# Graph attention layers on one core: normed rows turned by VectorE blocks and a DRAM scratch instead of by TensorE

## The chip, the cores and the metric

The kernel runs on one core of one Trainium2 chip. The metric is the device time of one execution in microseconds (us). TensorE (PE) multiplies and loads its weights (PEld), VectorE (DVE) and ScalarE (ACT) work on SBUF and PSUM, GpSimd (POOL) on SBUF alone, and SyncE (SP) only issues transfers here.

## The reference

64 graphs of 128 nodes with 256 features. The input is normed and clipped at zero, goes through three attention layers, and is added to the result:

```python
h = jnp.maximum(_layernorm(x, axis=-1), 0.0)          # x: (64, 128, 256)
x = h
for l in range(3):
    si = x @ attn_w[l, :d];  sj = x @ attn_w[l, d:]
    scores = si[:, :, None] + sj[:, None, :] + attn_b[l]
    scores = jnp.where(scores >= 0, scores, 0.2 * scores)
    scores = jnp.where(mask, scores, -jnp.inf)        # mask: adjacency or diagonal
    attn = jax.nn.softmax(scores, axis=-1)
    agg = jnp.einsum('bij,bjd->bid', attn, x)
    h = layernorm(x + agg, g1[l], beta1[l])
    ff = jax.nn.gelu(h @ W1[l] + b1[l], approximate=False) @ W2[l] + b2[l]
    x = layernorm(h + ff, g2[l], beta2[l])            # W1: 256x1024, W2: 1024x256
return x_input + x
```

## The kernel before

The work is cut into 48 items: 16 groups of four graphs (512 rows), each through three layers. A batch is four groups; its four groups go through layer 0, then layer 1, then layer 2, so a batch has 12 items and there are four batches. Item q has layer `q % 12 // 4`.

Each engine runs a list written out by hand: a prologue for the first items, then `slot(s)` for s from 1 on, in which the engine does pieces of the items s-1 to s+4. Engines are tied by counting semaphores only, and each engine works strictly in the order of its list. The order around the change is set by these lists.

For one item: `j_dots` and `i_dots` (VectorE, L620 and L627) make sj and si; sj goes to a DRAM scratch (`send_sj`) and comes back as a row on all 128 partitions (`load_sj`, tile `sj_bc`). `masked` (L654) takes the minimum of that row and a penalty tile `pen` of plus or minus 1e30 made from the adjacency by `penalty` (L641). `leaky` (ScalarE, L842) adds si and applies the slope, `minus_max` (VectorE, L658) reduces the maximum, `exps` (ScalarE, L848) makes the exponentials E, `e_turn` (TensorE, L1000) transposes them into the PSUM bank `util`, `et_out` copies them out, `aggregate` (L969) multiplies with x into an accumulator, `attend` (VectorE, L667) divides by the sum and adds x. `moments1` and `norm1` (L674, L517, L519, L680) norm the rows; between them GpSimd makes the reciprocal root as a power (`make_rstd`, L389). `z1_turn` (TensorE, L990) transposes the normed rows into `util` in two halves of four transposes. `h_high` (ScalarE) scales and shifts the half in place (`h_out`, L829) and rounds it to `ht_hi` (L836); `h_low` (VectorE, L685) makes the remainder `ht_lo`. The feed-forward part works in eight chunks: `ffn1(c)` (L940, 6 matmuls of 512 columns into one of three banks `hbank`), `gelu_high` (ScalarE, L813 and L819), `low` (VectorE, L541), `ffn2(c)` (L955, 12 matmuls of 256 columns into the accumulator). GpSimd makes gamma and beta times the normed rows (`h_gamma`, L409, `h_beta`, L416), VectorE adds them to the accumulator (`residual`, L555), norms (`moments2`, `norm2`, L562, L570), and GpSimd applies `x_gamma`, `x_beta` (L426, L434) and, in layer 2, `add_input` (L455). Items of layer 0 also need the input statistics (`input_moments`, L528, `input_shift`, L535) and `penalty`.

All eight PSUM banks are taken: three `hbank`, one `util`, and four `acc`, two for items of even q and two for those of odd q:

```python
acc = [psum(f"acc{i}", [P, HG, D]) for i in range(4)]
def acc_of(i, h): return acc[2 * (i.q % 2) + h]
```

So the aggregation of one item runs into the pair that ffn2 of the item before doesn't use. Weights are split in a high and a low part (`round_weights` on ScalarE, `split_weights`, L510, on VectorE) during the first items.

## Time and profile before

| | |
|---|---|
| Median of three runs | 1281.47 us (1281.34 to 1281.74) |
| The profiled execution, its own time | 1281.6 us |
| Its span, first to last instruction | 1279.8 us |
| Granted TensorE clock, mean | 0.997 |
| Busy: TensorE / weight loads | 1240.6 / 1122.5 us |
| Busy: VectorE / ScalarE / GpSimd | 1110.3 / 917.7 / 652.5 us |
| DMA | 52.31 MB, mean 41 GB/s |

The span leaves out what lies before the first and after the last instruction, 1.8 us here. Busy shares are means over the whole span. A matmul's duration reaches over the start of the next one, so the step from start to start, not the duration, is what a matmul costs.

### The profile page before, as it was taken

The numbers are of one execution on the slowest core, as the hardware profiler recorded it, in microseconds if no ns is written. First come the engines' busy times: TensorE is split into PE (matmuls) and PEld (weight loads), VectorE is DVE, ScalarE is ACT, GpSimd is POOL, SyncE is SP. The second block draws the span as 40 slices with busy tenths as digits, with TensorE's granted clock in tenths as the row PEclk, the third lists the DMA queues.
The fourth block names the chain that finished last, engine by engine and source line by source line (L and its number), as shares of the span: only waits on it lengthen the run. The fifth ranks groups of instructions, "written<-read, shape, count | busy, mean of one in ns | idle before, by whom it ended". The sixth has DMA issues, their size and how long they took to land.

```text
span 1279.8 us, 23042 instructions
## 1 busy us (share of the span) xinstructions
PE 1240.6 (97%) x7877; PEld 1122.5 (88%) x7877; DVE 1110.3 (87%) x3331; ACT 917.7 (72%) x1754; POOL 652.5 (51%) x535
## 2 busy tenths in 40 slices
PE   3899999999999999999999999999999999999997
PEld 1799999988899999999889999999989899989996
DVE  7888888899998788889998888789999888888765
ACT  4777777677876776678777776777778766776663
POOL 1435553556555534554566445544666355435563
PEclk9999999999999999999999999999999999999998
DMA  7111111112220001011230000002321100000111
GB/s 248 53 33 43 26 26 34 34 51 66 67 67 10 10 10 17 10 34 51 75 100 26 9 18 10 9 10 43 99 75 42 34 10 9 10 17 26 26 41 58
DMA packets 52944, 52.31 MB, mean 41 GB/s; under 512 B 9272, under 2 KB 45148, under 8 KB 52828
## 3 DMA queue, kind: packets, MB, share of 16 engines
q1 hardware_dynamic: 52828, 50.85, 14.4%
q8 instruction: 62, 1.02, 0.3%
q14 instruction: 54, 0.44, 0.1%
HBM read 42.36 MB, written 8.48 MB: 40 GB/s over the span
## 4 chain that ended last, share of the span: by engine, by line
PE 77%; DVE 18%; ACT 2%; issue 2%; DMA 1%; POOL 0%; DVEq 0%; POOLq 0%
PE acc L955 35%; PE hbank L940 33%; PE acc L969 5%; DVE hid_lo L541 3%; PE util L990 3%; DVE xs L680 2%; PE util L1000 1%; DVE xs L667 1%; DVE st L528 1%; DVE st L674 1%; DVE ve L519 1%; DVE mv L517 1%; DVE st L562 1%; DVE junk L627 1%; DVE sc L654 1%
## 5 line engine op out<-in xcount | busy, mean ns | idle before, releaser
L955 PE MATMUL acc<-w2hi,hid_hi 128*128 128x256 f32 x1536 | 446.0, 290 | 0.0
L813 ACT ACTIVATE hbank<-hbank,vec 128x512 f32<-128x512 f32 x384 | 253.7, 661 | 266.5 <-PE hbank L940 262.0
L955 PE MATMUL acc<-w2hi,hid_lo 128*128 128x256 f32 x1536 | 434.9, 283 | 0.0
L955 PE MATMUL acc<-w2lo,hid_hi 128*128 128x256 f32 x1536 | 434.4, 283 | 0.0
L389 POOL TENSOR_TENSOR rstd<-ve,halfs 128x4 f32<-128x4 f32 x111 | 120.1, 1082 | 492.1 <-DVE ve L519 487.2
L940 PE MATMUL hbank<-ht_hi,w1hi 128*128 128x512 f32 x768 | 311.2, 405 | 2.8 <-DVE hid_lo L541 1.4
L955 PEld LDWEIGHTS acc<-w2hi,hid_hi 128*128 128x128 f32 x1536 | 293.8, 191 | 10.5
L940 PE MATMUL hbank<-ht_lo,w1hi 128*128 128x512 f32 x768 | 302.6, 394 | 0.0
L955 PEld LDWEIGHTS acc<-w2lo,hid_hi 128*128 128x128 f32 x1536 | 293.7, 191 | 8.8
L940 PE MATMUL hbank<-ht_hi,w1lo 128*128 128x512 f32 x768 | 300.8, 392 | 0.0
L955 PEld LDWEIGHTS acc<-w2hi,hid_lo 128*128 128x128 f32 x1536 | 293.5, 191 | 0.0
L541 DVE TENSOR_TENSOR hid_lo<-hbank,hid_hi 128x512 fp32r<-128x512 f32 x384 | 257.5, 683 | 26.5 <-ACT hid_hi L819 24.7
L819 ACT CAST hid_hi<-hbank 128x512 fp32r<-128x512 f32 x384 | 225.6, 587 | 13.7 <-PE acc L955 1.7
L409 POOL TENSOR_TENSOR hb<-xs,ln_rows 128x512 f32<-128x512 f32 x96 | 128.9, 1343 | 87.2 <-DVE xs L680 87.2
L940 PEld LDWEIGHTS hbank<-ht_hi,w1lo 128*128 128x128 f32 x768 | 144.7, 188 | 32.6
L940 PEld LDWEIGHTS hbank<-ht_hi,w1hi 128*128 128x128 f32 x768 | 145.7, 190 | 25.6 <-DVE ht_lo L685 2.1
L940 PEld LDWEIGHTS hbank<-ht_lo,w1hi 128*128 128x128 f32 x768 | 145.9, 190 | 19.9
L685 DVE TENSOR_TENSOR ht_lo<-util,ht_hi 128x512 fp32r<-128x512 f32 x96 | 66.2, 689 | 95.1 <-ACT ht_hi L836 95.1
L416 POOL TENSOR_TENSOR hb<-hb,ln_rows 128x512 f32<-128x512 f32 x96 | 124.5, 1298 | 0.0
L680 DVE TENSOR_SCALAR xs<-xs,mv,rstd 128x256 f32<-128x256 f32 x192 | 112.0, 646 | 1.0 <-POOL rstd L389 0.9
L829 ACT ACTIVATE util<-util,vec 128x512 f32<-128x512 f32 x96 | 72.4, 754 | 36.1 <-PE util L990 35.9
L426 POOL TENSOR_TENSOR xs<-xs,ln_rows 128x512 f32<-128x512 f32 x64 | 82.7, 1292 | 23.4 <-DVE xs L570 23.4
(76 smaller groups left out, 1740.3 us busy)
## 6 DMA issues: line engine op xcount, KB each, us to landing
sj_bc<-sj_dram SPq DMA_DIRECT2D x47, 256.0 KB, 3.9
xraw<-in_x_dram SPq DMA_DIRECT2D x16, 512.0 KB, 4.4
out_dram<-xout SPq DMA_DIRECT2D x32, 256.0 KB, 4.4
xres<-in_x_dram SPq DMA_DIRECT2D x15, 512.0 KB, 5.6
xout<-in_L_gnn_W_dram SPq DMA_DIRECT2D x10, 512.0 KB, 5.0
adji<-in_adj_dram SPq DMA_DIRECT2D x16, 256.0 KB, 2.9
ln_rows<-in_L_gnn_g_dram SPq DMA_DIRECT2D x2, 384.0 KB, 8.0
ln_rows<-in_L_gnn_beta_dram SPq DMA_DIRECT2D x2, 384.0 KB, 7.6
```

The lines of the kernel that those rows point to most:

```text
L389: pool.tensor_tensor(rstd[n][:], ve[n][:], halfs[:], ALU.pow).then_inc(rstd_n[n], 1)
L409: pool.tensor_tensor(hb[:, i.q % 2, gs], x_of(i)[:, gs], rows_of(ln1_rows[:, 0], i.l), ALU.mult).then_inc(hgam_n, 1)
L416: pool.tensor_tensor(t, t, rows_of(ln1_rows[:, 1], i.l), ALU.add).then_inc(hb_n, 1)
L426: pool.tensor_tensor(t, t, rows_of(ln2_rows[:, 0], i.l), ALU.mult).then_inc(gam_n, 1)
L541: dve.tensor_tensor(hid_lo[:, k % HID], hbank[k % HB][:], hid_hi[:, k % HID].bitcast(F32), ALU.subtract).then_inc(lo_n, 1)
L680: dve.tensor_scalar(x_of(i)[:, g], x_of(i)[:, g], mv["1"][:, g, 0:1], rstd["1"][:, g:g + 1], ALU.subtract, ALU.mult).then_inc(z1_n, 1)
L685: dve.tensor_tensor(ht_lo[:, i.q % 2, m], util[:], ht_hi[:, i.q % 2, m].bitcast(F32), ALU.subtract).then_inc(htlo_n, 1)
L813: act.activation(hbank[k % HB][:], hbank[k % HB][:], ACT.Gelu, bias=b1c(i.l, c)).then_inc(gelu_n, 1)
L819: act.copy(hid_hi[:, k % HID], hbank[k % HB][:]).then_inc(hi_n, 1)
L829: act.activation(util[:], util[:], ACT.Identity, bias=beta1c(i.l, m), scale=g1c(i.l, m)).then_inc(ht_n, 1)
L940: mm = pe.matmul(hbank[k % HB][:], w[:, i.l, m, at_c], v[:, i.q % 2, m], start=m == 0 and n == 0, stop=m == KD - 1 and n == 2)
L955: mm = pe.matmul(to, v[:, k % HID, of_g], w[:, i.l, c], start=c == 0 and n == 0 and g % HG == 0, stop=c == C - 1 and n == 2, skip_group_ch ...
```

## The change

Seven things change at once.

- The normed rows of items 2 to 47 are no longer transposed by TensorE. VectorE transposes 32x32 blocks (`turn_z`, one instruction on 128x1024 into `tz`), one transfer writes `tz` to a DRAM scratch (`send_z`, 512 KB), and four transfers read it back with the blocks in their places (`move_z`, 128 KB each, contiguous pieces of 512 B). `h_out` reads that tile `zt` from SBUF and writes to `util`. Items 0 and 1 (`BY_PE = 2`) go on as before.
- `e_turn` writes to the bank into which the same item's aggregation goes afterwards. The four accumulator banks become two of `acc`, for ffn2, and two of `mix`, for E and the aggregation.
- `masked` becomes four instructions, each the sum of penalty and row with its maximum; the penalty becomes 0 or less, by a second instruction. `minus_max` takes that maximum, adds si, and applies the slope to 128x4 values, before `leaky` has run; it reduces nothing.
- The addition of epsilon to the variances moves from VectorE to GpSimd, into `make_rstd`.
- The attention bias is the starting value of the sum in `i_dots`; `add_bias` goes. `input_shift` becomes one instruction.
- sj goes to the scratch graph by graph (`[2, GG, P]`, elements of 4 B), and the row comes back contiguous for each graph.
- The lists of all engines are written anew. Attention of an item now runs one slot earlier, and inputs are loaded one or two slots earlier.

The new lists for a slot s, in their order, with t = item s-1, f = s, b = s+1, a = s+2, d = s+3, p = s+4, n = s+5 (what stands in brackets only for items of layer 0, or of layer 2 for the output):

- VectorE: residual(t,0), minus_max(a), residual(t,1), moments2(t), low(f,2), [penalty(n)], [input_shift(p)], norm2(t,0), low(f,3), norm2(t,1), attend(a,0), low(f,4), h_low(b,0), attend(a,1), low(f,5), moments1(a), j_dots(d), h_low(b,1), low(f,6), i_dots(d), low(f,7), norm1(a), [input_moments(n)], turn_z(a), low(b,0), masked(d), low(b,1).
- ScalarE: exps(a), gelu_high(f,3), et_out(a), gelu_high(f,4), h_high(b,0), gelu_high(f,5), [first_x(p)], h_high(b,1), gelu_high(f,6), (f,7), (b,0), (b,1), (b,2), leaky(d).
- TensorE: ffn1(f,3), (f,4), ffn2(f,0), (f,1), e_turn(a), ffn1(f,5), aggregate(a), ffn2(f,2), ffn1(f,6), (f,7), ffn2(f,3), (f,4), (f,5), ffn1(b,0), (b,1), (b,2), ffn2(f,6), (f,7).
- GpSimd: h_gamma(b) twice, make_rstd 2(t), x_gamma(t) twice, x_beta(t) twice, h_beta(f,0), make_rstd 1(a), h_beta(f,1), [add_input(t) twice], [make_rstd 0(n)].
- SP: send_sj(d), [load_xres(t)], load_sj(d), send_z(a), [load_adj(s+6)], move_z(a), [send_out(t,0)], [load_xraw(s+6)], [send_out(t,1)].

The diff of the rest, cut to its core:

```diff
+BY_PE = 2
+QD = 32
+NQ = P // QD
+MOVES = 16 * NQ
+MOVES_Z = MOVES
...
+tz = sb("tz", [P, KD * NQ, GG, QD])
+zt = sb("zt", [P, KD, NQ, GG, QD])
+sj_bc = sb("sj_bc", [P, GG, P])
+z_dram = nc.dram_tensor("z_dram", [P, KD * NQ * GG * QD], F32).ap()
+sj_dram = nc.dram_tensor("sj_dram", [2, GG, P], F32).ap()
...
-acc = [psum(f"acc{i}", [P, HG, D]) for i in range(4)]
+acc = [psum(f"acc{i}", [P, HG, D]) for i in range(HG)]
+mix = [psum(f"mix{i}", [P, HG, D]) for i in range(HG)]
 util = psum("util", [P, TOK])
 
-def acc_of(i, h): return acc[2 * (i.q % 2) + h]
+def acc_of(i, h): return acc[h]
+def mix_of(i, h): return mix[h]
...
+def wait_z_turned(eng, q):
+    if q < BY_PE:
+        eng.wait_ge(zt_n, KD * (q + 1))
+    else:
+        eng.wait_ge(tz_n, moved(q))
...
     def send_sj(i):
+        if i.q == 0:
+            return
         sp.wait_ge(dotj_n, i.q + 1)
         wait(sp, sj_in, 16 * (i.q - 2))
-        sp.dma_start(sj_dram[i.q % 2], dots[:, 1]).then_inc(sj_sent, 16)
+        sp.dma_start(sj_dram[i.q % 2].rearrange("g j -> j g"), dots[:, 1],
+                     allow_slow_non_contiguous=True).then_inc(sj_sent, 16)
 
     def load_sj(i):
+        if i.q == 0:
+            return
         sp.wait_ge(sj_sent, 16 * i.q)
         sp.wait_ge(mask_n, i.q)
-        sp.dma_start(sj_bc[:].rearrange("p j g -> p (j g)"),
-                     sj_dram[i.q % 2].rearrange("j g -> (j g)").partition_broadcast(P)).then_inc(sj_in, 16)
+        sp.dma_start(sj_bc[:].rearrange("p g j -> p (g j)"),
+                     sj_dram[i.q % 2].rearrange("g j -> (g j)").partition_broadcast(P)).then_inc(sj_in, 16)
+
+    def send_z(i):
+        if i.q < BY_PE:
+            return
+        sp.wait_ge(tz_n, moved(i.q))
+        wait(sp, zt_in, MOVES_Z * (moved(i.q) - 1))
+        sp.dma_start(z_dram, tz[:].rearrange("p c g t -> p (c g t)")).then_inc(z_sent, 16)
+
+    def move_z(i):
+        if i.q < BY_PE:
+            return
+        sp.wait_ge(z_sent, 16 * moved(i.q))
+        sp.wait_ge(ht_n, KD * i.q)
+        for b in range(NQ):
+            sp.dma_start(zt[b * QD:(b + 1) * QD].rearrange("p m a g t -> p m a (g t)"),
+                         z_dram.rearrange("(a p) (m b f) -> b p m a f", a=NQ, b=NQ, m=KD)[b]).then_inc(zt_in, 16)
...
     def make_rstd(n, q):
         if n == "2" and q == ITEMS - 1:
             return
-        pool.wait_ge(ve_n[n], q + 1)
+        pool.wait_ge(mv_n[n], GG * (q + 1))
         if n == "0":
             wait(pool, x0_n, GG * q)
+        pool.tensor_scalar(ve[n][:], mv[n][:, :, 1], EPS, None, ALU.add).then_inc(ve_n[n], 1)
+        pool.wait_ge(ve_n[n], q + 1)
         pool.tensor_tensor(rstd[n][:], ve[n][:], halfs[:], ALU.pow).then_inc(rstd_n[n], 1)
...
-        dve.wait_ge(mv_n[n], GG * (q + 1))
-        dve.tensor_scalar(ve[n][:], mv[n][:, :, 1], EPS, None, ALU.add).then_inc(ve_n[n], 1)
...
     def input_shift(i):
         dve.wait_ge(rstd_n["0"], i.g + 1)
         wait(dve, x0_n, GG * i.g)
-        for g in range(GG):
-            dve.tensor_scalar(nmr0[:, g:g + 1], mv["0"][:, g, 0:1], rstd["0"][:, g:g + 1], -1.0,
-                              ALU.mult, ALU.mult).then_inc(nmr0_n, 1)
+        dve.scalar_tensor_tensor(out=nmr0[:], in0=mv["0"][:, :, 0], scalar=-1.0, in1=rstd["0"][:],
+                                 op0=ALU.mult, op1=ALU.mult).then_inc(nmr0_n, 1)
...
     def i_dots(i):
         dve.wait_ge(dotj_n, i.q + 1)
-        for g in range(GG):
-            last = dve.tensor_tensor_reduce(junk[:, g], x_of(i)[:, g], attn_rows[:, i.l, 0], 1.0, 0.0,
-                                            ALU.mult, ALU.add, dots[:, 0, g:g + 1])
+        wait(dve, leaky_n, GG * (i.q - 1))
+        wait(dve, below_n, i.q - 1)
+        for g in range(GG):
+            last = dve.tensor_tensor_reduce(junk[:, g], x_of(i)[:, g], attn_rows[:, i.l, 0], 1.0,
+                                            attn_bias[:, i.l:i.l + 1], ALU.mult, ALU.add,
+                                            si_of(i)[:, g:g + 1])
         last.then_inc(dots_n, 1)
-
-    def add_bias(i):
-        dve.wait_ge(dots_n, i.q + 1)
-        wait(dve, leaky_n, GG * i.q)
-        dve.tensor_scalar(si[:], dots[:, 0], attn_bias[:, i.l:i.l + 1], None, ALU.add).then_inc(si_n, 1)
...
-                                 op0=ALU.mult, op1=ALU.add).then_inc(pen_n, 1)
+                                 op0=ALU.mult, op1=ALU.add).then_inc(edge_n, 1)
+        dve.wait_ge(edge_n, i.g + 1)
+        dve.tensor_scalar(pen[:, i.g % PENS], pen[:, i.g % PENS], 0.0, None, ALU.min).then_inc(pen_n, 1)
 
     def masked(i):
         dve.wait_ge(pen_n, i.g + 1)
-        wait(dve, et_n, i.q)
+        wait_e_turned(dve, i.q - 1)
         if i.q == 0:
             dve.wait_ge(sj_n, 1)
             row = util[:].rearrange("p (g j) -> p g j", g=GG)
         else:
             dve.wait_ge(sj_in, 16 * i.q)
-            row = sj_bc[:].rearrange("p j g -> p g j")
-        dve.tensor_tensor(sc[:], pen[:, i.g % PENS], row, ALU.min).then_inc(mask_n, 1)
+            row = sj_bc[:]
+        for g in range(GG):
+            last = dve.tensor_tensor_reduce(sc[:, g], pen[:, i.g % PENS, g], row[:, g], 1.0, -BIG, ALU.add,
+                                            ALU.max, msj[:, g, 0:1])
+        last.then_inc(mask_n, 1)
 
     def minus_max(i):
-        dve.wait_ge(leaky_n, GG * (i.q + 1))
-        dve.tensor_reduce(negm[:], sc[:], AX_X, ALU.max, negate=True).then_inc(negm_n, 1)
+        dve.wait_ge(mask_n, i.q + 1)
+        dve.wait_ge(dots_n, i.q + 1)
+        wait(dve, exp_n, GG * i.q)
+        dve.scalar_tensor_tensor(out=below[:, :, 0], in0=msj[:, :, 0], scalar=-1.0, in1=si_of(i), op0=ALU.mult,
+                                 op1=ALU.subtract).then_inc(below_n, 1)
+        dve.wait_ge(below_n, i.q + 1)
+        dve.scalar_tensor_tensor(out=negm[:], in0=below[:, :, 0], scalar=SLOPE, in1=below[:, :, 0], op0=ALU.mult,
+                                 op1=ALU.min).then_inc(negm_n, 1)
+
+    def turn_z(i):
+        if i.q < BY_PE:
+            return
+        dve.wait_ge(z1_n, GG * (i.q + 1))
+        wait(dve, z_sent, 16 * (moved(i.q) - 1))
+        dve.transpose(tz[:], x_of(i).rearrange("p g (c j) -> p c g j", j=QD)).then_inc(tz_n, 1)
...
     def h_out(i, m):
-        act.wait_ge(zt_n, KD * i.q + m + 1)
-        if i.q == 0 and m == 0:
-            act.wait_ge(vec_ready, 1)
-        act.activation(util[:], util[:], ACT.Identity, bias=beta1c(i.l, m),
-                       scale=g1c(i.l, m)).then_inc(ht_n, 1)
+        if i.q < BY_PE:
+            act.wait_ge(zt_n, KD * i.q + m + 1)
+            if i.q == 0 and m == 0:
+                act.wait_ge(vec_ready, 1)
+            act.activation(util[:], util[:], ACT.Identity, bias=beta1c(i.l, m),
+                           scale=g1c(i.l, m)).then_inc(ht_n, 1)
+        else:
+            act.wait_ge(zt_in, MOVES_Z * moved(i.q))
+            act.wait_ge(htlo_n, KD * i.q + m)
+            act.activation(util[:].rearrange("p (g a t) -> p a g t", g=GG, a=NQ), zt[:, m], ACT.Identity,
+                           bias=beta1c(i.l, m), scale=g1c(i.l, m)).then_inc(ht_n, 1)
...
-            pe.wait_ge(y1_n, GG * (i.q + 1))
+            wait(pe, y2_n, 2 * i.q)
...
     def e_turn(i):
-        if i.q > 0:
-            pe.wait_ge(exp_n, GG * (i.q + 1))
-        wait(pe, htlo_n, KD * i.q)
-        for g in range(GG):
-            if i.q == 0:
-                pe.wait_ge(exp_n, g + 1)
-            mm = pe.transpose(util[:, g * P:(g + 1) * P], sc[:, g], ident[:])
+        wait(pe, y1_n, GG * (i.q - 1) + HG)
+        turned = mix[0][:].rearrange("p g d -> p (g d)")
+        for g in range(GG):
+            pe.wait_ge(exp_n, GG * i.q + g + 1)
+            mm = pe.transpose(turned[:, g * P:(g + 1) * P], sc[:, g], ident[:])
         mm.then_inc(et_n, 1)
```

## Rows read from the trace of the kernel before

**Rows 1.** The page's busy times.
```profile
PE 1240.6 (97%) x7877; PEld 1122.5 (88%) x7877; DVE 1110.3 (87%) x3331; ACT 917.7 (72%) x1754; POOL 652.5 (51%) x535
```

**Rows 2.** Windows: A:B us, PE, PEld, DVE, ACT, POOL busy us, clock, DMA.
```profile
439.52:465.07 25.55, 25.55 (x166) 23.26 (x165) 21.34 (x66) 18.25 (x35) 12.47 (x10) 1.00 0.04 12
593.58:619.91 26.33, 26.29 (x167) 23.62 (x167) 26.03 (x80) 20.20 (x39) 15.80 (x13) 1.00 0.26 81
```

**Rows 3.** Timeline of VectorE: start us, us, engine, line; first norms.
```profile
233.36 2.35 DVE L680 TENSOR_SCALAR xs<-xs,mv,rstd 128x256 f32<-128x256 f32 x4
541.83 2.36 DVE L680 TENSOR_SCALAR xs<-xs,mv,rstd 128x256 f32<-128x256 f32 x4
```

**Rows 4.** Timeline of TensorE around one turn of normed rows.
```profile
701.05 0.60 PE L990 MATMUL util<-ident,xs 128*128 128x128 f32 x4
701.40 0.48 PE L940 MATMUL hbank<-ht_hi,w1hi 128*128 128x512 f32 x1
701.72 0.39 PE L940 MATMUL hbank<-ht_lo,w1hi 128*128 128x512 f32 x1
701.95 0.40 PE L940 MATMUL hbank<-ht_hi,w1lo 128*128 128x512 f32 x1
```

**Rows 5.** Groups of instructions: busy us, mean ns; idle before.
```profile
L389 POOL TENSOR_TENSOR rstd<-ve,halfs 128x4 f32<-128x4 f32 x111 | 120.1, 1082 | 492.1 <-DVE ve L519 487.2
L519 DVE TENSOR_SCALAR ve<-mv 128x4 f32<-128x4 f32 x111 | 38.4, 346 | 3.8
L658 DVE TENSOR_REDUCE negm<-sc 128x4 f32<-128x512 f32 x48 | 32.4, 676 | 1.8 <-ACT sc L842 1.8
L654 DVE TENSOR_TENSOR sc<-pen,sj_bc 128x512 f32<-128x512 bf16 x47 | 51.0, 1085 | 0.4 <-DMA sj_bc<-sj_dram 0.4
L620 DVE CUSTOM_DVE_ANT_0 junk<-xs,attn_rows 128x256 bf16<-128x256 f32 x192 | 81.0, 476 | 0.6 <-ACT xs L862 0.4
L510 DVE TENSOR_TENSOR w1lo<-xout,w1hi 128x1024 fp32r<-128x1024 f32 x6 | 7.3, 1218 | 0.7 <-ACT w1hi L808 0.7
L641 DVE SCALAR_TENSOR_TENSOR pen<-adji,diag 128x512 bf16<-128x512 int32 x16 | 12.0, 750 | 0.0
L541 DVE TENSOR_TENSOR hid_lo<-hbank,hid_hi 128x512 fp32r<-128x512 f32 x384 | 257.5, 683 | 26.5 <-ACT hid_hi L819 24.7
```

**Rows 6.** Timeline: VectorE instructions alone and beside a GpSimd one.
```profile
26.35 1.38 DVE L680 TENSOR_SCALAR xs<-xs,mv,rstd 128x256 f32<-128x256 f32 x4
...
37.13 2.35 POOL L394 TENSOR_TENSOR ln_rows<-ln_rows,hb 128x768 f32<-128x768 f32 x1
38.20 1.83 DVE L641 SCALAR_TENSOR_TENSOR pen<-adji,diag 128x512 bf16<-128x512 int32 x1
...
598.28 1.33 DVE L519 TENSOR_SCALAR ve<-mv 128x4 f32<-128x4 f32 x1
598.29 1.30 POOL L409 TENSOR_TENSOR hb<-xs,ln_rows 128x512 f32<-128x512 f32 x1
...
722.73 2.36 DVE L680 TENSOR_SCALAR xs<-xs,mv,rstd 128x256 f32<-128x256 f32 x4
723.54 1.40 POOL L409 TENSOR_TENSOR hb<-xs,ln_rows 128x512 f32<-128x512 f32 x1 [1.71 <-DVE xs L680]
```

**Rows 7.** DMA issues: count, KB each, median us to landing.
```profile
sj_bc<-sj_dram SPq DMA_DIRECT2D x47, 256.0 KB, 3.9
xres<-in_x_dram SPq DMA_DIRECT2D x15, 512.0 KB, 5.6
adji<-in_adj_dram SPq DMA_DIRECT2D x16, 256.0 KB, 2.9
sj_dram<-dots SPq DMA_DIRECT2D x47, 2.0 KB, 1.4
```

**Rows 8.** Groups of ScalarE's exponentials.
```profile
L848 ACT ACTIVATE sc<-sc,negm 128x128 f32<-128x128 f32 x192 | 74.9, 392 | 2.2 <-DVE negm L658 1.7
L848 ACT ACT_TABLE_LOAD x46 | 59.0, 1283 | 0.8
```

More of the change, by code:

```diff
@@ L218, in raw, with si_of @@
             return xraw, xraw_in, 16 * (i.g + 1 if i.q == 0 else i.g + 1 - EARLY)
+        def si_of(i):
+            return dots[:, 2 * (i.q % 2)]
         def x_of(i):
@@ new lines, in load_xres, with send_out @@
+            def load_xres(i):
+                if i.q == ITEMS - 1:
+                    return
+                wait(sp, out_ready, 2 * i.g)
+                if i.g == 0:
+                    sp.wait_ge(ln1_ready, 1)
+                sp.dma_start(xres[:], group(x, i.g)).then_inc(xres_in, 16)
+            def send_out(i, h):
+                if i.q == ITEMS - 1:
+                    return
+                gs = slice(h * HG, (h + 1) * HG)
+                sp.wait_ge(out_ready, 2 * i.g + h + 1)
+                sp.dma_start(group(out, i.g)[:, gs], xout[:, i.g % 2, gs]).then_inc(out_sent[i.g % 2], 16)
@@ L338, in _ @@
+            i1, i2, i3 = (item(q) for q in range(1, 4))
             load_xraw(item(0))
@@ L706, in slot @@
                 if f:
-                    low(f, 2)
-                if b:
-                    moments1(b)
-                if f:
                     low(f, 3)
-                if d and d.l == 0:
-                    penalty(d)
                 if t:
@@ L716, in slot @@
                 if a:
-                    masked(a)
-                if b:
-                    norm1(b)
+                    attend(a, 0)
                 if f:
                     low(f, 4)
-                if p and p.l == 0:
-                    input_moments(p)
                 if b:
                     h_low(b, 0)
+                if a:
+                    attend(a, 1)
                 if f:
                     low(f, 5)
+                if a:
+                    moments1(a)
+                if d:
+                    j_dots(d)
+                if b:
+                    h_low(b, 1)
+                if f:
                     low(f, 6)
+                if d:
+                    i_dots(d)
+                if f:
                     low(f, 7)
                 if a:
-                    minus_max(a)
+                    norm1(a)
+                if n and n.l == 0:
+                    input_moments(n)
+                if a:
+                    turn_z(a)
                 if b:
-                    h_low(b, 1)
+                    low(b, 0)
                 if d:
-                    j_dots(d)
-                if p and p.l == 0:
-                    input_shift(p)
-                if f:
-                    residual(f, 0)
-                split_weights(s + 4)
+                    masked(d)
+                if b:
+                    low(b, 1)
             i0, i1, i2, i3 = (item(q) for q in range(0, 4))
@@ L1005, in slot @@
                 if f:
-                    ffn2(f, 6)
-                    ffn2(f, 7)
+                    ffn1(f, 3)
+                    ffn1(f, 4)
+                    ffn2(f, 0)
+                    ffn2(f, 1)
+                if a:
+                    e_turn(a)
+                if f:
+                    ffn1(f, 5)
+                if a:
+                    aggregate(a, 0)
+                    aggregate(a, 1)
+                if f:
+                    ffn2(f, 2)
+                    ffn1(f, 6)
+                    ffn1(f, 7)
+                    ffn2(f, 3)
+                    ffn2(f, 4)
+                    ffn2(f, 5)
                 if b:
```

393 lines of the change are left out of this document (194 added, 199 removed).

## The prediction

> **What bounds the kernel now.** I read the page's busy shares first, then the windows of single items, then the order of instructions on TensorE and on VectorE, then the list of waits. The page says TensorE is busy for 97% of the span and VectorE for 87% [rows 1]. An average hides two kinds of item, so I cut four periods out, each from the first norm of one item to that of the next (L680). A quiet item takes 25.55 us; TensorE is busy all of it, VectorE for 21.34 us. A heavy item, whose four look-ahead neighbours are in layer 0 (input statistics, penalty) while layer 2 sends output, takes 26.3 us, and VectorE is busy for 26.0 us of it [rows 2]. Quiet items are bound by TensorE, heavy ones by VectorE. There are four heavy items at each of the three places where a batch of 12 items ends and the next begins, 12 in all. They cost little today because VectorE may run behind and catch up: from the norm at 233.36 to that at 541.83, 12 items, 308.47 us pass [rows 3], against 12 x 25.58 = 306.96 (25.58 is the usual step between two such norms, give or take 0.03), so 1.5 us are lost for a batch, 4.5 us in three.
>
> **TensorE: what goes.** The change takes both transposes of the normed rows (L990) off TensorE for 46 of 48 items; the first two keep them. Their busy time is not their price, since matmuls overlap. From one start to the next: the transposes start at 701.05 and the next matmul at 701.40, and that one delays its successor to 701.72, 0.32 us where such starts elsewhere are 0.23 apart (701.72 to 701.95). So 0.35 + 0.09 = 0.44 us. The item's second turn has the same two gaps [rows 4]. An item saves 0.88 us and its TensorE period falls from 25.58 to 24.70; 46 items save 40.5 us. E's four transposes stay and only change banks, so they cost what they did. TensorE's idle time before L990 is mostly in the prologue, whose first two items keep these transposes, so I gain nothing there.
>
> **VectorE: what goes and comes, for one quiet item.** Consecutive instructions overlap by a little under 0.1 us, so I take means and round down. Gone: the two additions of epsilon (L519, 0.35 on average with the held ones in it; I take 0.2 each), the bias addition of the same size (0.2), the reduction for the maximum (L658, 0.6) and the single mask instruction (L654, 1.0): 2.2 us. Come: two dependent instructions on 128x4, each like L519, 0.4; four masked sums with a maximum, of 128x128, the operation of L620, which takes 0.48 us at 256 elements [rows 5]. Half the elements cost between half of that less the overlap and all of it less the overlap: 0.16 to 0.40 each; I take 0.22, 0.9 in all. And the block turn of 128x1024 (`turn_z`), which the trace doesn't have. The nearest row in size is L510, 128x1024 in 1.22 us. A floor is half of it (two elements for one), a ceiling twice it, 2.4, as its operand is read in strips and no row shows what blocks cost. I take 1.2, because L510 moves as many elements. Sum +2.5, net +0.3: 21.34 becomes 21.6 us, under the 24.70 that TensorE needs.
>
> **VectorE beside GpSimd.** Some VectorE instructions are held while a large GpSimd instruction runs. The third or fourth L680 costs an extra 1 us: four take 2.35 us, although 26.35 shows four in 1.38 with GpSimd idle, and GpSimd's L409 starts inside them. L519 took 1.33 us beside L409, and L641 1.83 beside L394, while the other fifteen L641 take (12.0 - 1.83) / 15 = 0.68 [rows 5, 6]. The instructions that read PSUM (L541, L667) show no such thing. A quiet item has one hold, a heavy one three. The Trainium skill (SBUF — State Buffer, "Who interferes with whom") says that a VectorE instruction in a two-port mode, or with two SBUF inputs against a GpSimd instruction that reads SBUF, is held for the whole of the other. By that rule the masked sums and both small instructions of the new maximum join those that can be held, which speaks against the change: three holds more would make quiet items 24.6 and heavy ones 28.2 us. The trace agrees for L641, which has two inputs; for a small one only L519 shows it.
>
> A heavy item now: 26.03 + 0.3, less the held L519 that leaves (1.2), less three of four small shifts (0.4), plus a second pass over the penalty (0.2 to 0.6, as 128x512 bf16; nearest is L641; I take 0.5): 25.2. The new order puts both norms, j_dots and i_dots near GpSimd's now unbroken run of x_gamma and x_beta, 4 x 1.3 us by L409, so I add one hold: 26.2. Bounds 25.2 and 27.2.
>
> **GpSimd** gets the additions of epsilon, 111 small instructions, between 0.3 us (twice L519) and 1.1 us (rstd, L389) each. It has half its time free [rows 1, 5]. But after moments2 VectorE now has only one subtraction (0.6) before norm2 in a quiet item, and the chain epsilon plus power takes about 0.3 + 1.0 + 0.2: some 0.7 us of wait, again inside VectorE's 3 us of spare. In heavy items penalty and shift cover it. In GpSimd's own queue h_gamma now stands ahead of this pair, 2 x 1.3 us, but it ends before moments2 does.
>
> **The long way of the rows.** A turned item leaves by one 512 KB transfer and returns by four of 128 KB in 512 B pieces. Nearest rows: 512 KB in 5.6 us; for the pieces the mask input, 256 KB in rows of 512 B, 2.9 us; twice as many pieces in four issues: 4 to 6 us [rows 7]. With the waits between them, 10 to 12 us, for which SP's queue holds load_adj's 256 KB in between; what stands behind the wait for the first transfer there (the output and the next input) has more than half an item of cover. In its slot `turn_z` has behind it on VectorE only two low (L541) and the mask: 21.6 less 2 x 0.6 less 0.9 is 19.5, plus some 1.1 us of waits, so it ends near 20.6 us. `h_high` comes in ScalarE's next slot behind the maximum (1.0), two table loads (2 x 1.28), four exponentials (1.6), and two GELU chunks and E's copy, 3.0: ScalarE's 18.25 us for an item less 2.6 and 1.6 leaves 14.1 for what amounts to 11.5 chunks, 1.2 each [rows 2, 5, 8]. So 24.7 + 8.2 = 32.9. The cover is 12.3 us. It just holds; if it were late, ScalarE and VectorE, both in order, would stand behind it. Bound: 0 to 3 us per item.
>
> The sj row is now written as 512 elements of 4 B instead of 128 of 16 B. It took 1.4 us; with the pieces of the mask input as ceiling, 2.9; then 3.9 for the broadcast [rows 7]. From j_dots to masked VectorE has 6.3 us plus its waits, in place of half a slot: 6.9 us can end 0.5 us late, within the spare. The Trainium skill (DMA: Bandwidth & Descriptors, "Rules for kernel authors") says that a non-contiguous last dimension makes one descriptor of each element. No row here shows such a write. Taken with the 512 pieces it gives the same 2.9 us.
>
> **The accumulator.** ffn2 now has two banks instead of four, so its first chunk waits for both residuals of the item before. TensorE covers with two ffn1 chunks, 2 x 6 x 0.23 = 2.76 us [rows 4]; VectorE needs 0.6 (a residual, like L541) + 0.4 + 0.6 and a release, 1.7 us, if it is on time. So VectorE may be behind by 1 us only, where before it could be behind by 3; heavy items are no longer made up for. If GpSimd's h_gamma, released by the first residual, holds the two small instructions in between, 1.3 us are added and TensorE stands 0.3 us per item.
>
> **The sum.** Against the profiled execution's own 1281.6 us (span 1279.8; the median of the runs is 1281.47, which I treat as the same): 1281.6 - 40.5 - 4.5 = 1236.6 if TensorE never waits. Heavy items: 12 x (26.2 - 24.7) = 18, less 1 us of tolerance at each of three places: +15. Quiet items: 34 x 0.1 for small waits: +4 rounded. Prologue and tail: the order changes, but first GELU, sj transfers and weight splits queue as before: 0, with 3 us either way. Total 1255.6, say 1256 us.
>
> **Rivals.** (a) Fewer holds, heavy items at 25.2 or less and TensorE bound nearly throughout: 1236.6 + 12 x 0.5 - 3 = 1240. For it: the held L519 goes. (b) The single accumulator pair: small instructions held beside h_gamma, 0.3 to 0.6 us of stall on each of 46 items: 1256 + 14 to 28, about 1275. For it: h_gamma starts just when these do; against: they may be through first. (c) The other side: the transfers through DRAM come late. The point is a return of about 14 us, past which ScalarE stands, VectorE's spare is used up and each us costs 46 us; at 15 us, 1256 + 46 = 1302, slower. For it: two dependent transfers with the adjacency, input and output between them, in heavy items above all; against: every 512 KB row lands within 6 us. (d) Nothing gained, since VectorE sets the pace in every item: it needs 25.6 us instead of 21.6 + waits, thus a block turn at 2.4 us and two more holds: 1280 to 1283.
>
> **Chances.** Forecast 0.45 (own range 1246 to 1268), (a) 0.15, (b) 0.17, (c) 0.17, (d) 0.06. The range reaches to (a) and past (b) up to the edge of (c): 1238 to 1290; what lies outside is mostly (c). No change means within 0.2%, 2.6 us, about what a measurement of this kernel can tell: faster 0.75 (forecast, (a), most of (b)), same 0.06 (most of (d)), slower 0.19 ((c) and the ends of (b) and (d)).
>
> **What would show it.** Quiet items 24.7 us long with TensorE busy throughout, no L990 after the prologue; the block turn 1.1 to 1.3 us; heavy items near 26.2 with VectorE full. Wrong: idle TensorE before ffn2 released by a residual (b), idle ScalarE before `h_out` released by a transfer into zt (c), masked waiting for sj_bc, or quiet items over 25 us.

## The result and the profile after

The changed kernel takes 1553.09 us, the median of four runs (1551.38 to 1558.33), beside 1281.53 us for the kernel before (1281.34 to 1281.74). The ratio is 1.213, 95% interval 1.210 to 1.216: slower by 272 us, where 25 us less was forecast. The profiled execution took 1551.38 us, with a span of 1549.6 us and a mean granted clock of 0.915 (before: 0.997).

The page of the kernel after: the busy times and, from its part 4, the chain that ended last, by engine and by line.

```profile
PE 1292.6 (83%) x7509; PEld 1152.1 (74%) x7509; DVE 1061.1 (68%) x3568; ACT 925.1 (60%) x1754; POOL 674.0 (43%) x648
...
DMA 43%; PE 30%; DVE 24%; issue 2%; ACT 1%; DVEq 0%; POOL 0%; SPq 0%; ACTq 0%; POOLq 0%
DMA sj_dram<-dots 27%; DMA sj_bc<-sj_dram 14%; PE hbank L1059 13%; PE acc L1074 12%; DVE hid_lo L616 5%; DVE xs L758 5%; DVE st L765 4%; DVE junk L695 3%; PE mix L1088 3%; DVE sc L730 2%; DVE ht_lo L777 2%; PE mix L1113 1%; DVE mv L595 1%; DMA adji<-in_adj_dram 1%; DVE msj L730 0%
```

No engine is full. TensorE went from 97% of the span to 83% [rows 1], VectorE from 87% to 68%, and 43% of the chain is transfers: 27% is the 2 KB write of sj, 14% the broadcast that brings it back. The waits show where that is paid; the columns are total us, times and the longest one.

```profile
DVE sc L730 <- DMA sj_bc<-sj_dram: 314.3, 47, 8.5
ACT sc L948 <- DVE msj L730: 290.1, 48, 9.0
PEld hbank L1059 <- DVE hid_lo L616: 223.8, 45, 7.1
PE hbank L1059 <- DVE hid_lo L616: 204.6, 45, 6.6
```

This is one stall seen three times. In each of 47 items `masked` stands 314.3 / 47 = 6.7 us for the row of sj. ScalarE's `leaky` waits for `masked`. Behind `masked` in VectorE's list stands `low(b,1)`, on which TensorE's next chunk depends. The DMA issues, with the median us to landing, and then SP's own waits, show why the row is late:

```profile
z_dram<-tz SPq DMA_DIRECT2D x46, 512.0 KB, 5.6
zt<-z_dram SPq DMA_DIRECT2D x184, 128.0 KB, 2.8
sj_bc<-sj_dram SPq DMA_DIRECT2D x47, 256.0 KB, 4.8
```

```profile
SPq L347 <- DMA sj_dram<-dots: 395.6, 47, 10.3
SPq L363 <- DMA z_dram<-tz: 215.8, 46, 8.0
```

Before issuing the broadcast (L347) SP waits 8.4 us in each item for the 2 KB that go to `sj_dram`. The view of the line that issues them (L339) has their time to landing, which was 1.4 us before [rows 7]:

```profile
DMA to landing us min/median/max: 8.0/9.0/10.9
```

One item in the timelines of VectorE and SP, where the last bracket is idle time and what ended it:

```profile
708.40 0.42 DVE L695 CUSTOM_DVE_ANT_0 junk<-xs,attn_rows 128x256 bf16<-128x256 f32 x1
...
715.35 1.21 DVE L749 STREAM_TRANSPOSE tz<-xs 128x1024 f32<-128x1024 f32 x1
716.49 0.65 DVE L616 TENSOR_TENSOR hid_lo<-hbank,hid_hi 128x512 fp32r<-128x512 f32 x1
722.22 0.29 DVE L730 CUSTOM_DVE_ANT_0 sc<-pen,sj_bc 128x128 f32<-128x128 bf16 x1 [5.08 <-DMA sj_bc<-sj_dram]
```

```profile
708.85 0.37 SPq L339 DMA_DIRECT2D sj_dram<-dots  x1
717.03 0.34 SPq L347 DMA_DIRECT2D sj_bc<-sj_dram  x1
717.47 0.38 SPq L355 DMA_DIRECT2D z_dram<-tz  x1
```

`j_dots` ends at 708.8 and the write is issued at once; 8.2 us later it has landed, and the broadcast needs 5.2 more. VectorE was ready for it at 717.14: in this item the cover, the time that VectorE fills with other work, is 8.3 us, and the chain takes 13.4. The cover is that long in 15 of the 47 items, in the first three and where input statistics fall into the gap; in the other 32 it is 6.7 us. Over all 47 it is 7.2 us, and the chain 13.9.

The transfer takes next to no time on the DMA engines. Another such write is issued at 1367.24, and SP goes on at 1377.20, when it has landed. In a window over nearly the whole of that (the last three columns are granted clock, DMA share and GB/s), the engines are 3% busy. In finer slices all of that lies before 1369, and from then on they move nothing:

```profile
1367.00:1377.00 10.00, 10.00 (x69) 9.23 (x68) 6.92 (x19) 4.35 (x7) 1.69 (x2) 1.00 0.03 0
```

The stall has a second price. Three neighbouring windows in which TensorE stands and starts again:

```profile
1405.00:1410.00 5.00, 4.47 (x31) 3.83 (x30) 0.14 (x1) 1.42 (x3) 0.00 (x0) 1.00 0.08 21
1410.00:1415.00 5.00, 1.78 (x7) 1.30 (x8) 3.34 (x15) 2.39 (x5) 1.10 (x1) 0.94 0.50 168
1415.00:1420.00 5.00, 5.00 (x32) 4.92 (x32) 3.17 (x12) 4.64 (x13) 3.98 (x5) 0.72 0.27 77
```

TensorE waits 3.75 us, until 1413.2, and the granted clock falls just after it has resumed: 0.94, then 0.72, then back to 1.00 from 1420 on. Part of the stretch thus ran at the lower level of 1.2 GHz: in the timeline the matmuls of 256 columns start 0.12 us apart before the stop, 0.21 from 1415.0 to 1417.5, and 0.12 again from 1417.9.

### The profile page after: what moved, and what is told of

It is laid out like the page before. It is cut to its first block, busy times and chain, and to the rows that moved or that the text cites. A ratio compares the mean times of both kernels' runs of the same rounds, so it can differ in the third digit from the quotient of the medians.

```text
span 1549.6 us, 23072 instructions
## 1 busy us (share of the span) xinstructions
PE 1292.6 (83%) x7509; PEld 1152.1 (74%) x7509; DVE 1061.1 (68%) x3568; ACT 925.1 (60%) x1754; POOL 674.0 (43%) x648
## 4 chain that ended last, share of the span: by engine, by line
DMA 43%; PE 30%; DVE 24%; issue 2%; ACT 1%; DVEq 0%; POOL 0%; SPq 0%; ACTq 0%; POOLq 0%
DMA sj_dram<-dots 27%; DMA sj_bc<-sj_dram 14%; PE hbank L1059 13%; PE acc L1074 12%; DVE hid_lo L616 5%; DVE xs L758 5%; DVE st L765 4%; DVE junk L695 3%; PE mix L1088 3%; DVE sc L730 2%; DVE ht_lo L777 2%; PE mix L1113 1%; DVE mv L595 1%; DMA adji<-in_adj_dram 1%; DVE msj L730 0%
## 5 line engine op out<-in xcount | busy, mean ns | idle before, releaser
L1059 PE MATMUL hbank<-ht_hi,w1hi 128*128 128x512 f32 x768 | 329.0, 428 | 212.6 <-DVE hid_lo L616 204.6
L1074 PE MATMUL acc<-w2lo,hid_hi 128*128 128x256 f32 x1536 | 452.0, 294 | 0.0
L1074 PEld LDWEIGHTS acc<-w2hi,hid_hi 128*128 128x128 f32 x1536 | 316.2, 206 | 11.3 <-issue 1.7
L488 POOL TENSOR_TENSOR hb<-xs,ln_rows 128x512 f32<-128x512 f32 x96 | 121.3, 1284 | 465.7 <-DVE xs L630 398.9
L1074 PEld LDWEIGHTS acc<-w2lo,hid_hi 128*128 128x128 f32 x1536 | 314.9, 205 | 8.9
L1059 PE MATMUL hbank<-ht_lo,w1hi 128*128 128x512 f32 x768 | 319.7, 416 | 0.0
L1059 PE MATMUL hbank<-ht_hi,w1lo 128*128 128x512 f32 x768 | 319.2, 416 | 0.0
L1074 PEld LDWEIGHTS acc<-w2hi,hid_lo 128*128 128x128 f32 x1536 | 312.2, 203 | 0.0
L730 DVE CUSTOM_DVE_ANT_0 sc<-pen,sj_bc 128x128 f32<-128x128 bf16 x188 | 51.3, 328 | 314.3 <-DMA sj_bc<-sj_dram 314.3
L948 ACT ACTIVATE sc<-sc,dots 128x128 f32<-128x128 f32 x192 | 61.3, 390 | 290.1 <-DVE msj L730 290.1
L758 DVE SCALAR_TENSOR_TENSOR xs<-mix,rden,xs 128x256 f32<-128x256 f32 x192 | 83.7, 478 | 66.2 <-PE mix L1088 66.0
```

Of the source, the lines that this page charges most:

```text
L488: pool.tensor_tensor(hb[:, i.q % 2, gs], x_of(i)[:, gs], rows_of(ln1_rows[:, 0], i.l), ALU.mult).then_inc(hgam_n, 1)
L730: last = dve.tensor_tensor_reduce(sc[:, g], pen[:, i.g % PENS, g], row[:, g], 1.0, -BIG, ALU.add, ALU.max, msj[:, g, 0:1])
L758: dve.scalar_tensor_tensor(out=x_of(i)[:, g], in0=mix_of(i, h)[:, g % HG], scalar=rden[:, g:g + 1], in1=x_of(i)[:, g], op0=ALU.mult, op1=A ...
L1059: mm = pe.matmul(hbank[k % HB][:], w[:, i.l, m, at_c], v[:, i.q % 2, m], start=m == 0 and n == 0, stop=m == KD - 1 and n == 2)
L1074: mm = pe.matmul(to, v[:, k % HID, of_g], w[:, i.l, c], start=c == 0 and n == 0 and g % HG == 0, stop=c == C - 1 and n == 2, skip_group_ch ...
```

## The experiments

Times are medians of four runs, and their ratios are to the kernel before run beside them (1281.9 to 1282.2 us); where it says a single run, there is one time.

**The row of sj node by node, as before; everything else as after.** The mask reads the row with a step of four elements instead.

```diff
-sj_dram = nc.dram_tensor("sj_dram", [2, GG, P], F32).ap()
+sj_dram = nc.dram_tensor("sj_dram", [2, P, GG], F32).ap()
-sp.dma_start(sj_dram[i.q % 2].rearrange("g j -> j g"), dots[:, 1], ...)
+sp.dma_start(sj_dram[i.q % 2], dots[:, 1])
-row = sj_bc[:]
+row = sj_bc[:].rearrange("p j g -> p g j")
```

> The changed kernel with one thing taken back: sj goes to the scratch node by node (128 pieces of 16 B) and the mask reads the row with a step of 16 B, as before the change. Theory A, the 512 pieces of 4 B are the cause: the write of sj lands in 1.4 us instead of 9.0, VectorE's wait for sj_bc (314.3 us) falls under 30, TensorE's granted clock goes back over 0.98, and the time is what the prediction forecast without it, 1250 to 1275 us. Theory B, the transfers of the turned rows crowd the queue and sj waits behind them: the write still lands in 6 us or more and the time stays over 1450. Theory C, two accumulator banks instead of four hold TensorE: sj lands fast, but TensorE then stands before ffn2 and the time is 1300 to 1400.

Measured: 1243.11 us (1242.83 to 1243.44), ratio 0.970 (0.968 to 0.971), clock 0.996, and the wait of `masked` is nearly gone. The write lands in 1.7 us, and no wait of TensorE for the accumulator appears, so Theory A stands; its time is 7 us under the range I gave. Of this kernel: the busy times, that wait, and the windows of a quiet and of a heavy item, from block turn to block turn.

```profile
PE 1199.8 (97%) x7509; PEld 1084.6 (87%) x7509; DVE 1078.8 (87%) x3568; ACT 919.5 (74%) x1754; POOL 676.0 (54%) x648
```

```profile
DVE sc L729 <- DMA sj_bc<-sj_dram: 4.1, 6, 0.9
```

```profile
445.51:470.16 24.65, 24.65 (x158) 22.47 (x157) 21.00 (x71) 18.42 (x36) 12.77 (x12) 1.00 0.18 54
595.20:619.95 24.75, 24.75 (x158) 22.35 (x157) 23.42 (x84) 20.06 (x40) 17.24 (x18) 1.00 0.41 128
```

The books close: the wait of `masked` shrinks by 314.3 - 4.1 = 310.2 us, and the time by 1553.1 - 1243.1 = 310.0 (308.6 between the spans of the profiled executions). For TensorE, 216 of the 309 us of span are less idle time (257.0 to 41.2) and 93 less busy time (1292.6 to 1199.8) for the same 7509 matmuls. This version beats both kernels.

The step in the mask's reading isn't free. The rows of the masked sums in this run, in the changed kernel, and of the mask of the kernel before with the row graph by graph (the next run):

```profile
L729 DVE CUSTOM_DVE_ANT_0 sc<-pen,sj_bc 128x128 f32<-128x128 bf16 x188 | 68.2, 417 | 4.2 <-DMA sj_bc<-sj_dram 4.1
```

```profile
L730 DVE CUSTOM_DVE_ANT_0 sc<-pen,sj_bc 128x128 f32<-128x128 bf16 x188 | 51.3, 328 | 314.3 <-DMA sj_bc<-sj_dram 314.3
```

```profile
L655 DVE TENSOR_TENSOR sc<-pen,sj_bc 128x512 f32<-128x512 bf16 x47 | 32.6, 693 | 84.0 <-DMA sj_bc<-sj_dram 84.0
```

Medians are 0.38 us with the step of 16 B and 0.29 contiguous, and the one mask instruction of before took 1.09 with the step [rows 5] against 0.69 without: 0.4 us an item either way. In quiet items VectorE has that to spare, as the doubled block turn below shows.

**The kernel before, with the row graph by graph alone.** The same three edits, the other way.

```diff
-sp.dma_start(sj_dram[i.q % 2], dots[:, 1])
+sp.dma_start(sj_dram[i.q % 2].rearrange("g j -> j g"), dots[:, 1], ...)
```

> The kernel before with only the sj row changed to graph by graph (512 pieces of 4 B, contiguous row for the mask). Theory A: the write lands in about 9 us although there is no other new transfer; with half an item of cover (the mask comes some 14 us after j_dots) the time moves by less than 1%, 1278 to 1290 us, and L654 falls from 1.09 to 0.7 us. Theory B: the write lands in under 3 us, since nothing crowds it.

Measured: 1324.75 us (1323.29 to 1326.83), ratio 1.034 (1.032 to 1.035). The write is as slow in the old order (SP waits 407.1 us in 45 items for it), but `masked` waits only 84.0 us in 45 items, as it stands later in the old list. So the row graph by graph costs 43 us in the old order and 310 in the new one, although the mask itself falls to 0.69 us as expected. I had expected less than 8 us: the old order's cover falls short of 9.0 + 5.1 us, too, by 84.0 / 45 = 1.9 us.

**After, with the normed rows turned by TensorE in all items.** The bank `util` takes them again, late in the slot.

```diff
-BY_PE = 2
+BY_PE = 48
 aggregate(a, 1)
+z1_turn(b, 0)
 ffn2(f, 2); ffn1(f, 6)
+z1_turn(b, 1)
```

> The changed kernel with all turns of normed rows back on TensorE (its two L1105 turns for every item, no block turn, no scratch), sj still graph by graph. Theory A: the write of sj still lands in 9 us and the mask waits as long; TensorE's 0.88 us are lost in time in which it stands anyway, so 1530 to 1570 us. Theory B: without those transfers sj lands in under 4 us and the time falls under 1400.

Measured: 1654.24 us, ratio 1.291 (1.289 to 1.293); the mask waits 380.4 us, and SP 426.8 us for the 2 KB. With no 1 MB to and from DRAM per item the small write is no faster, so it is not crowded out by the rows. My range ended at 1570, 84 us too low. ScalarE waits 119.5 us for the turns here; how they and the late row build on each other I have not taken apart.

**Small writes by themselves, first attempt.** The kernel before, plus one write in each item in one of seven shapes.

> The kernel before with one more transfer for each item, issued when the sj row has landed, in turn of seven kinds, to read the time to landing by itself: 512 pieces of 4 B graph by graph, 128 of 16 B, 256 of 8 B, 512 of 4 B spaced 8 B apart, 512 of 4 B spaced 256 B apart, 512 of 512 B, and 512 of 4 B read from DRAM. If it is the number of pieces: 512 of 512 B land no sooner than 512 of 4 B, about 9 us. If it is writing less than 512 B: those take 3 to 4 us, all 4 B writes 9, 256 of 8 B about 5, and the read is quick. If it is neighbours in one line of DRAM: the spaced ones are quick.

A single run, 1287.63 us. All shapes signalled the same semaphore, and the trace gave no landing for a single one. Nothing follows from it.

**The row as before and the rows turned by TensorE, at early places.** This leaves the rest of the change: new order, mask, banks, epsilon.

```diff
-BY_PE = 2
+BY_PE = 48
 ffn1(f, 3)
+z1_turn(b, 0)
 ...
 ffn2(f, 2)
+z1_turn(b, 1)
```

> The changed kernel with sj node by node, and the turns of the normed rows back on TensorE for every item, in places of TensorE's list where it would otherwise start a chunk (after ffn1(f,3) and after ffn2(f,2)). What is left of the change is all but the turn and the row. If the turn's price is the 0.88 us an item of the prediction, the time is 1243.1 + 46 x 0.88 = 1284 us, the same as before the change, and the rest of the change is worth nothing by itself. If the new lists and the lighter VectorE gain by themselves, it is under 1270; if h_out now waits for TensorE in its place, over 1295.

Measured: 1291.32 us (1290.83 to 1291.46), ratio 1.007 (1.006 to 1.009), where 1284 us was expected. Against 1243.11, taking the turns off TensorE is worth 48.2 us, 1.05 for each of 46 items. The rest of the change, as the turns stand here in TensorE's list, costs 9 us. The period between two copies of E in quiet items (421.0 to 446.7 to 472.4) is 25.7 us with the turns, and 24.65 without.

**The same with the late places of the 1654 us kernel.**

> As the one before, with the two turns later in TensorE's list (after aggregate and after ffn1(f,6)), the places of the run with all turns on TensorE and sj graph by graph, which took 1654 us. If those 100 us over the changed kernel came from the places, this one is 20 to 100 us slower than the kernel with the early places; if they came only together with the slow row, the two are within 10 us.

A single run, 1296.2 us. The places matter by 5 us when the row is quick. Against 1243.11 the turns at these places cost 53 us; of the 101 us by which the 1654 us kernel lies above the changed one, the other 48 come only together with the late row. ScalarE waits 112.2 us for the turns here too, so that wait alone doesn't explain them.

**The row in pairs.** Two graphs go together: 256 pieces of 8 B.

```diff
-sj_dram = ... [2, P, GG]
+sj_dram = ... [2, 2, P, 2]
-sp.dma_start(sj_dram[i.q % 2], dots[:, 1])
+sp.dma_start(sj_dram[i.q % 2].rearrange("h j e -> j h e"), dots[:, 1].rearrange("p (h e) -> p h e", h=2))
```

> The changed kernel with sj written in 256 pieces of 8 B (two graphs together, the mask reads with a step of 8 B). If the landing grows with the number of pieces it is about 4 us, 2.5 us later than with 128 of 16 B; VectorE then waits some 2 us an item at the mask, of which about 2 are covered by the idle time it has anyway: 1245 to 1290 us. If it is a fixed price of pieces under 16 B, it lands in 9 us and the time is 1550.

Measured: 1259.87 us, ratio 0.983 (0.981 to 0.984), inside the range expected; the write lands in 3.2 us, and the mask waits 46.3 us in 39 items. Half the pieces cost a third of the time, so the price isn't a fixed one per piece. Reading the row with a step of 8 B leaves the masked sums at 0.29 us.

**Small writes by themselves, each with its own semaphore.** One form per item:

```python
dma_start(pd[0].rearrange("g j -> j g"), src)            # L322: 4 B, graph by graph, as after
dma_start(pd[1], src)                                    # L324: 128 x 16 B, as before
dma_start(pd[3][:, :, 0], src)                           # L328: 4 B, 8 B apart
dma_start(pd[4][:, :, 0], src)                           # L330: 4 B, 256 B apart
dma_start(pd[5].rearrange("g j e -> j g e"), rows)       # L332: 512 x 512 B
dma_start(pd[6][:, :, 0].rearrange("g j -> j g"), src)   # L334: 4 B, graph by graph, 64 B apart
```

> The kernel before with one more transfer for each item from item 8 on, issued when the sj row has landed, and each of its eight kinds with a semaphore of its own, so that its landing can be read. 4 B graph by graph: 9 us if the price belongs to that write alone. 128 of 16 B: 1.5. 256 of 8 B: 3 to 5. If it is the number of small pieces, 4 B with 8 B, 64 B or 256 B between them take 9 us as well; if it is that neighbours in DRAM come from different partitions and wait for one another, those with 64 and 256 B between them take 2 to 3 us. 512 of 512 B: 3 us. 512 of 4 B read from DRAM: 2 to 3 us.

A single run, 1286.51 us. The views of L322 and L334, two of the lines that issue them:

```profile
DMA to landing us min/median/max: 8.8/9.1/11.5
...
DMA to landing us min/median/max: 1.8/1.9/2.3
```

Medians of all: 9.1 us as after; 2.1 for 128 pieces of 16 B; 3.3 for 256 of 8 B; 4.7 for 4 B elements 8 B apart; 2.1 for 256 B apart; 1.9 for 64 B apart; 2.3 for 512 pieces of 512 B; 1.9 for reading 4 B elements from DRAM. The same number of 4 B elements, from the same partitions, lands in 1.9 us if they don't lie near each other. So neither the count nor the size makes it slow by itself; it takes neighbours. Each median is of five writes, and one form differs by up to 1.1 us between this run and the last one below.

**After with the row as before, plus an idle 2 KB write graph by graph for which the broadcast also waits.** Nothing reads it.

```diff
 sp.dma_start(sj_dram[i.q % 2], dots[:, 1]).then_inc(sj_sent, 16)
+sp.dma_start(idle_dram[i.q % 2].rearrange("g j -> j g"), attn_rows[:, 0, 0, 0:GG], ...).then_inc(idle_sent, 16)
 ...
+sp.wait_ge(idle_sent, 16 * i.q)
```

> The kernel with sj node by node (1243.1 us), plus a write of 512 pieces of 4 B graph by graph of constant data to a scratch that nobody reads, issued right behind the write of sj; the load of the row waits for both. Theory A, the landing of that write alone is the loss: 1535 to 1570 us, the time of the changed kernel (1553.1), although row and mask are as in the quick one. Rival, the layout of the row matters otherwise (its read, the mask's operand): 1243 to 1300.

Measured: 1611.74 us, ratio 1.257 (1.255 to 1.259); SP waits 431.5 us in 47 for the idle write, the mask 343.9. Waiting for such a write brings the whole loss back, with the row itself laid out as in the 1243 us kernel; whether only the wait does it is the next question. The time is 42 to 77 us beyond what I expected, and 59 above the changed kernel. The idle write is issued 0.4 us after the row's, 19 us in 47 items, and the masked sums behind the stall take 0.38 us each in place of 0.29, some 17 us (estimates from these rows); the rest, some 23, stays open.

**The same write, without the wait.** The broadcast waits only for the idle write of the item before.

```diff
-sp.wait_ge(idle_sent, 16 * i.q)
+wait(sp, idle_sent, 16 * (i.q - 1))
```

> The same idle write, but the load of the row waits only for the idle write of the item before. Theory A, only the wait costs: within 0.5% of 1243.1 us. Rival, the pieces also hold up the transfers behind them in the queue or at the memory: sj_bc lands later than 4.1 us by some us, and the time is 1260 to 1500.

Measured: 1493.21 us (1492.33 to 1495.72), ratio 1.165 (1.163 to 1.167). The theory that only the wait costs fell: 250 of the 310 us are lost without it. SP's timeline and windows of one item (columns as above):

```profile
1016.10 0.66 SPq L342 DMA_DIRECT2D idle_dram<-attn_rows  x1
1017.53 0.33 SPq L351 DMA_DIRECT2D sj_bc<-sj_dram  x1
```

```profile
1020.00:1022.00 2.00, 2.00 (x10) 1.65 (x10) 1.96 (x8) 1.86 (x4) 0.00 (x0) 1.00 0.24 54
1022.00:1024.00 2.00, 2.00 (x17) 1.92 (x16) 2.00 (x7) 1.12 (x2) 1.27 (x2) 1.00 0.00 0
1024.00:1026.00 2.00, 2.00 (x16) 1.87 (x15) 0.00 (x1) 0.59 (x1) 0.00 (x0) 1.00 1.36 211
```

The broadcast is issued 1.4 us behind the idle write, and the mask begins at 1028.18, when the broadcast, 10.6 us after its issue, is reported landed. Its packets run until 1022 (54 GB/s here and 85 in the two us before, together about its 256 KB), then no DMA engine does anything for 2 us; what moves from 1024 on is the next transfer, issued at 1023.45. So such a write holds back the landing of what is issued behind it, too. The 512 KB write of the rows lands in 6.9 us here, and in 2.6 without the idle write.

**The block turn done twice, in the 1243 us kernel.**

```diff
+dve.transpose(tz[:], x_of(i).rearrange("p g (c j) -> p c g j", j=QD)).then_inc(tz2_n, 1)
```

> The kernel with sj node by node, with the block turn done twice, 1.25 us more of VectorE for each of 46 items. By the prediction a quiet item has 24.7 - 21.6 - waits, some 2 us of spare, so it stays at 24.65; a heavy one (24.75 now) is at its limit and takes up to 1.2 us more: 1243 + 12 x 1.2 = 1258, range 1248 to 1262. If VectorE has no spare in quiet items either: 1243 + 46 x 1.25 = 1300.

Measured: 1259.17 us (1259.06 to 1259.99), ratio 0.982 (0.981 to 0.984), as expected. Quiet items still take 24.65 us from turn to turn, so VectorE has at least 1.25 us to spare there; heavy ones take 26.00 in place of 24.75, and 12 x 1.25 = 15 of the 16 us are theirs.

**How near is a neighbour?** Eight more forms in the kernel before.

> Nothing of the computation is left out: the kernel before, with one additional small write to a scratch in DRAM per item from item 8 on, of which only the time from issue to landing counts. In program order the eight forms are: (0) 512 elements of 4 B graph by graph, dense; (1) node by node with 16 B from element to element; (2) node by node with 32 B; (3) one graph alone, 128 elements, dense; (4) 512 elements, dense, but the four neighbours of each 16 B come from one partition; (5) graph by graph with 32 B; (6) graph by graph with 16 B; (7) graph by graph with 8 B. Theory A, the time grows with how many elements are written separately into the same 64 B (16 of them gave 9.1 us, 8 gave 4.7, 1 gave 1.9): (0) 9.1, (1) and (6) about 3, (2) and (5) about 2.3, (3) 9 although it has a quarter of the elements, (4) 9, (7) 4.7. Theory B, the time grows with the number of crowded elements in the whole transfer: as A, but (3) 3 us. Theory C, only neighbours from different partitions are slow: as A, but (4) near 3. The kernel's time stays near 1286.

A single run, 1288.87 us. The medians, ordered by how many elements written separately fall into the same 64 B:

| in 64 B | form | us to landing |
|---|---|---|
| 16 | 512 elements, graph by graph | 10.2 |
| 16 | 128 elements, one graph alone | 7.7 |
| 16 | 512 elements, four neighbours from one partition | 7.1 |
| 8 | graph by graph, 8 B apart | 4.3 |
| 4 | graph by graph / node by node, 16 B apart | 2.7 / 3.8 |
| 2 | graph by graph / node by node, 32 B apart | 2.2 / 3.2 |
| 1 | graph by graph, 64 B apart (earlier run) | 1.9 |

The line that decides is the second: a quarter of the elements at the same density takes three quarters of the time. Theory A holds in its order, and roughly in size; from one to 16 it grows by about (10.2 - 1.9) / 15 = 0.55 us for each further element, less at first (4.3 us with eight) than at the end. Theory B (count) and C (only different partitions) fall as the whole cause, though both matter by 2 to 3 us. That the stretch is 64 B long isn't shown: with even spacing a longer stretch would give the same order. Why such writes take long isn't shown either; being served one after another would fit.

## Why the prediction was wrong

- **The sj row: the step that failed.** "It took 1.4 us; with the pieces of the mask input as ceiling, 2.9; then 3.9 for the broadcast", so "6.9 us can end 0.5 us late, within the spare", and the sum got no term for it. The write measured 9.0 us and the broadcast 4.8, 13.8 in all. The cover, 6.3 us and its waits, was right: it is 6.7 us in 32 items and 8.3 or a little more in 15, and past it `masked` stood 6.7 us an item on average. (The two terms make 6.8, not 6.9, which changes nothing.) The ceiling was borrowed from pieces of another kind: 512 B each, not 4 B, and read from DRAM, not written. I compared them by number and kB; what mattered most was how many separately written elements lie next to each other, here 16 in 64 B, from 16 partitions. Undone alone, the step gives back 310 us, more than the 297 by which the forecast was missed. The Trainium skill (DMA: Bandwidth & Descriptors, "Rules for kernel authors") warned of one descriptor for each element, and the packets agree: the page of the profile counts 31000 under 512 B after and 12952 with the row as before, 18048 more, which is 47 x (512 - 128). I priced it by their count. The Trainium skill (DMA: Bandwidth & Descriptors, "Specifications") says that below 512 B the DMA engine does read-modify-write. That would fit neighbours being served in turn; no run here shows it, and elements 64 B apart, as small, land in 1.9 us.
- **The rivals.** (c), "transfers through DRAM come late", had the right kind of mechanism and the right kind of arithmetic (past the cover each us is paid in every item), but was placed on the normed rows alone. I had treated the sj chain as hidden, so it was no rival. "masked waiting for sj_bc" stood among the signs of a wrong prediction, and it was that line.
- **TensorE's turns: right.** With the row as before, quiet items take 24.65 us, forecast 24.70. Taken by itself the turn is worth 48 to 53 us, by where the turns would stand in TensorE's list; 40.5 was forecast, and 4.5 for lost catching up.
- **VectorE, quiet items: right.** Block turn 1.21 to 1.25 us (1.2). Masked sums 0.21 us from start to start in the changed kernel (0.22), and 0.31 with the row as before, through the step in their reading. Busy 21.00 us for a quiet item (21.6), although `i_dots` rose by 0.07 each for its starting value (0.41 us from start to start, where `j_dots` takes 0.34 and both took 0.35 before), a term I had not counted.
- **Heavy items: mis-sized.** I gave them 26.2 us; they take 24.75 with VectorE busy for 23.42. The holds beside GpSimd mostly didn't come: the median L770 takes 0.404 us of the 192, the mean 0.424, so some four of them are held by 1 us, where in [rows 6] one in each four shown beside GpSimd was. With the row as before this is the case of rival (a), 1240 us, and 1243.1 were measured. The three further holds that the prediction worked out by the rule of the Trainium skill (SBUF — State Buffer, "Who interferes with whom"; heavy items at 28.2) didn't come either, but the rule isn't refuted: the instructions seldom meet. In the quiet item above GpSimd is idle while the masked sums run. In the whole run with the row as before, 10 of 188 masked sums overlap a large GpSimd instruction, and these take 0.72 to 1.48 us in place of 0.38, as it says. The second small instruction of the maximum overlaps one in 45 of 48 items, but starts first, and keeps its 0.16 us.
- **The way of the rows through DRAM: right to say it holds, too long in its parts.** With the row as before its transfers take 2.6 us out and 2.9 back. In one item `turn_z` runs from 470.16 to 471.4, the last of the four reads has left SP by 476.6, so that the way takes about 8 us, not 10 to 12, and `h_out` starts at 482.68. Nowhere is more than 2 us waited for `zt` in a whole run. The accumulator pair (b) costs nothing: no wait of TensorE for a residual is among the listed ones. VectorE waits 18.0 us in 20 items for the reciprocal root, 0.9 each (0.7).
- **What stays open.** How much of the 310 us the lower clock adds: TensorE's 93 us more of busy time lie partly where it would have stood anyway. Why the turns on TensorE cost 48 us more together with the late row than without it, and where some 23 us of the kernel with the awaited idle write go. And why neighbouring small writes land late at all.

## What to carry to other kernels

When a layout change turns one small write to DRAM into single elements, ask which elements end up next to each other and who writes them, not only how many there are; put the step on the reading side, where it cost VectorE 0.4 us an item here, and nothing measurable with a step of 8 B. If no row of the profile has the same direction, piece size and density, the honest bound is open upwards, and the step deserves a rival of its own: find the cover in us, and state what each us beyond it costs. And in a program where every engine keeps a fixed order, ask what stands behind the instruction that waits: the new order paid its 6.7 us in full, once for each item (314 us waited, 310 lost), while the old one lost 43 us of the 84 waited.
